# Cross-attention with LoRA, one core: value and denominator matmuls as one run, key stacks split for four heads and placed through memory

## The reference, cut to what matters

```python
# x (16, 112, 1024), ctx (16, 375, 1024); H = 1024, NH = 32 heads, NKV = 8 key heads, HD = 32, R = 16
def lora(x, W, A, B): return x @ W + 2.0 * (x @ A @ B)
q = lora(x, Wq, Aq, Bq)          # 32 heads of 32
k = lora(ctx, Wk, Ak, Bk)        # 8 heads of 32, each shared by 4 query heads
v = lora(ctx, Wv, Av, Bv)
scores = einsum('bhqd,bhtd->bhqt', q, k) / sqrt(32)
attn = softmax(scores, axis=-1)
context = einsum('bhqt,bhtd->bhqd', attn, v)
out = x + lora(context, Wo, Ao, Bo)
```

## Time and profile of the kernel before

| what | value |
|---|---|
| median of 3 runs | 1053.68 us (1049.55 to 1054.18) |
| the profiled execution | 1055.77 us, its span 1054.0 us |
| TensorE busy, matmuls / weight loads | 992.0 us (94%) / 783.7 us (74%) |
| VectorE, ScalarE, GpSimd busy | 583.9, 496.7, 286.2 us |
| mean granted clock of TensorE | 0.982 of full speed |
| chain of work that ended last | TensorE 79%, VectorE 7%, ScalarE 6% |

### The profile page before, as it was taken

One profiled execution on the slowest core, in us unless ns is written; L12 is line 12 of the kernel. 1 busy time (PEld: TensorE's weight loads), 2 busy tenths in 40 slices (PEclk: granted clock), 3 DMA queues, 4 the chain that ended last, 5 costly groups with the idle time before them and its releaser, 6 DMA issues.

```text
span 1054.0 us, 17987 instructions
## 1 busy us (share of the span) xinstructions
PE 992.0 (94%) x5904; PEld 783.7 (74%) x5904; DVE 583.9 (55%) x1005; ACT 496.7 (47%) x971; POOL 286.2 (27%) x84
## 2 busy tenths in 40 slices
PE   6989999999999999999999999999999857999998
PEld 5879999887777777777777777777777424678886
DVE  5661221387666666666666667666667555323331
ACT  3341221436656657666666666666667433201000
POOL 1201000002334434434433533533543435300000
PEclk9999999999999999999999999999999887999999
DMA  6729523462513513423323323324322340667652
GB/s 188 238 81 247 174 70 105 121 155 59 130 46 87 123 46 94 108 58 94 95 71 94 95 71 94 95 61 104 95 53 56 90 129 31 167 206 216 195 163 80
DMA packets 104436, 118.13 MB, mean 112 GB/s; under 512 B 29536, under 2 KB 89056, under 8 KB 104400
## 3 DMA queue, kind: packets, MB, share of 16 engines
q1 hardware_dynamic: 100540, 104.00, 37.2%
q10 hardware_dynamic: 3860, 13.67, 3.6%
HBM read 87.59 MB, written 29.82 MB: 111 GB/s over the span
## 4 chain that ended last, share of the span: by engine, by line
PE 79%; DVE 7%; ACT 6%; issue 4%; DMA 3%; ACTq 0%; SPq 0%; POOL 0%; DVEq 0%; POOLq 0%
PE ps L664 12%; PE ps L666 12%; PE ps L665 12%; PE ps L854 9%; PE ps L869 8%; PE ps L843 7%; PE ps L749 4%; PE ps L804 3%; PE ps L808 3%; PE ps L806 3%; PE ps L905 3%; ACT probs L1038 2%; ACT k_stack L978 1%; DVE ct_lo L1169 1%; DMA out_dram<-residual 1%
## 5 line engine op out<-in xcount | busy, mean ns | idle before, releaser
L1247 DVE TENSOR_REDUCE maxima<-ps 112x1 f32<-112x375 f32 x512 | 270.8, 543 | 107.6 <-PE ps L854 101.1
L1038 ACT ACTIVATE probs<-ps 125x448 f32<-125x448 f32 x384 | 206.9, 544 | 134.1 <-PE ps L843 130.3
L645 POOL TENSOR_TENSOR prob_sum<-probs 125x1792 f32<-125x1792 f32 x32 | 129.3, 4042 | 380.5 <-ACT probs L1038 380.5
L854 PE MATMUL ps<-k_stack,q_stack 96*112 96x376 f32 x512 | 188.9, 369 | 7.4 <-DVE maxima L1247 5.8
L843 PE MATMUL ps<-q_stack,k_stack 97*125 97x448 f32 x384 | 147.6, 385 | 13.8 <-ACT probs L1038 13.5
L854 PEld LDWEIGHTS ps<-k_stack,q_stack 96*112 96x112 f32 x512 | 90.5, 177 | 86.5 <-DVE maxima L1247 69.5
L650 POOL TENSOR_TENSOR prob_sum<-prob_sum,probs 125x1792 f32<-125x1792 f32 x32 | 129.1, 4033 | 34.4 <-ACT probs L1038 34.4
L978 ACT ACTIVATE k_stack<-ps 32x376 fp32r<-32x376 f32 x256 | 121.6, 475 | 9.9 <-PE ps L666 6.0
L804 PE MATMUL ps<-wv_hi,ct_hi 128*125 128x256 f32 x384 | 112.1, 292 | 0.5 <-DVE k_stack L1174 0.5
L808 PE MATMUL ps<-wv_hi,ct_lo 128*125 128x256 f32 x384 | 108.1, 281 | 0.0
L806 PE MATMUL ps<-wv_lo,ct_hi 128*125 128x256 f32 x384 | 108.0, 281 | 0.0
(11 more groups left out here) (80 smaller groups left out, 1477.0 us busy)
## 6 DMA issues: line engine op xcount, KB each, us to landing
ctx_in<-in_ctx_dram SPq DMA_DIRECT2D x16, 1344.0 KB
q_stack<-q_scratch SPq DMA_DIRECT2D x96, 224.0 KB, 3.6
x_in<-in_x_dram SPq DMA_DIRECT2D x8, 896.0 KB, 8.4
q_scratch<-q_out_hi SPq DMA_DIRECT2D x16, 448.0 KB, 2.8
q_scratch<-q_out_lo SPq DMA_DIRECT2D x16, 448.0 KB, 3.7
attn_scratch<-attn SPq DMA_DIRECT2D x32, 224.0 KB, 3.7
attn_rows<-attn_scratch SPq DMA_DIRECT2D x14, 512.0 KB, 4.6
inv_tile<-inv_scratch SPq DMA_DIRECT2D x56, 128.0 KB, 5.0
```

Of the source, the lines that this page charges most:

```text
L854: mm = pe.matmul(ps[0:NQ, NAT + i % 2, 0:NTE], qst[nxt][0:STK, g, rr * NQ:(rr + 1) * NQ], kst[nxt][0:STK, g, :], start=True, stop=True)
L1038: act.activation(probs[:, c, j, :], ps[0:TR, score_bank(i), 0:QH], ACT.Exp, scale=SM).then_inc(exp_done, 1)
L1247: dve.tensor_reduce(maxima[:, h, i:i + 1], ps[0:NQ, NAT + i % 2, 0:NT], AX.X, ALU.max).then_inc(max_done, 1)
```

## The change

1. The three P pieces and D of a half-batch become one P piece late in the half-batch (0.815 of its cost): 12 value matmuls in chunk order and then the four denominators of the same half-batch. D stays as the place where ScalarE copies the denominators and SP stores them, at the start of the next half-batch.
2. GpSimd adds `probs` per head: eight additions of 448 columns instead of two of 1792.
3. A half-batch's four key heads are split by one ScalarE copy and one VectorE subtraction over all 128 partitions into new tiles `k_out_hi`, `k_out_lo`. SP stores both to a new scratch in memory (`store_k`, at F0 and F1), waits for the stores, and loads the high part twice and the low part once into the stack (`load_k`, at G0 and G1). N of that half-batch waits for the loads. The stores of the second four heads come at the end of the second half-batch, their loads in the first half-batch after it.
4. The plan: S and N are due earlier, and S alternates between two banks from the first pair on.
5. ScalarE's wait for the stored queries moves ahead of the steps.

```diff
-S_IN_DEN = (3, 5, 7, 9, 11)
+S_IN_DEN = (1, 3, 5, 7, 9, 11)
 PLAN = sorted(
-    [("S", i, 0.01 + 0.07 * i) for i in range(TC * JH)]
-    + [("P", 0, 0.31), ("P", 1, 0.583), ("P", 2, 0.925), ("A", 0, 0.048), ("D", 0, 0.097)]
+    [("S", i, 0.01 + 0.065 * i) for i in range(TC * JH)]
+    + [("A", 0, 0.005), ("D", 0, 0.005), ("P", 0, 0.815)]
     + [("I", 0, 0.35), ("J", 0, 0.45)]
-    + [("N", i, 0.03 + 0.052 * i) for i in range(JH * RH)] + [("M", 0, 0.925)]
-    + [("E0", j, 0.62 + 0.08 * j) for j in range(JH)] + [("E1", j, 0.03 + 0.06 * j) for j in range(JH)]
-    + [("F0", j, 0.62 + 0.08 * j) for j in range(JH)] + [("F1", j, 0.03 + 0.06 * j) for j in range(JH)],
+    + [("N", i, 0.02 + 0.045 * i) for i in range(JH * RH)] + [("M", 0, 0.805)]
+    + [("E0", 0, 0.55), ("F0", 0, 0.55), ("G0", 0, 0.75), ("E1", 0, 0.82), ("F1", 0, 0.82), ("G1", 0, 0.12)],
...
+        if piece[0] == "K" and piece[2] == KC - 1:
+            early = [item for item in order if item[0] in (f"E{piece[1]}", f"F{piece[1]}", f"G{piece[1]}")]
+            order = [item for item in order if item not in early] + early
...
+            def store_k(b, half):
+                sp.wait_ge(k_lo_set, 2 * b + half + 1)
+                for hl, t in ((0, kev_hi[half]), (1, kev_lo[half])):
+                    sp.dma_start(k_scr[hl, bass.ds(b, 1), half, :, :].rearrange("b p n -> p (b n)"),
+                                 t[:, :].bitcast(F32)).then_inc(k_stored[half], 16)
+            def load_k(b, par, half):
+                sp.wait_ge(k_stored[half], 32 * (b + 1))
+                for n, hl in enumerate((0, 0, 1)):
+                    sp.dma_start(kst[par][HD * n:HD * (n + 1), half * JH:(half + 1) * JH, :].bitcast(F32),
+                                 k_scr[hl, bass.ds(b, 1), half, :, :].rearrange("b (j d) n -> d (b j) n", d=HD)
+                                 ).then_inc(k_in[half][par], 16)
...
+                        elif kind == "F0":
+                            store_k(b + 2, 0)
+                        elif kind == "G0":
+                            load_k(b + 2, off % 2, 0)
+                        elif kind == "F1":
+                            store_k(b + 2, 1)
+                        elif kind == "G1":
+                            load_k(b + 1, (off + 1) % 2, 1)
...
                             if i == 0:
                                 pe.wait_ge(q_in[h][nxt], 48 * (pair + (off + 1) // 2 + 1))
-                                pe.wait_ge(k_lo_set, JH * (m + 1))
+                                pe.wait_ge(k_in[h][nxt], 48 * (pair + (off + 1) // 2 + 1))
...
-                            pe.wait_ge(exp_done, NS * n + JH * (i + 1))
-                            if i == 0:
-                                at_least(pe, attn_set, n)
-                                pe.wait_ge(v_set, 2 * (b + 1))
-                            for j in range(JH):
...
-                        elif kind == "D":
-                            denominators(n - 1)
+                            pe.wait_ge(exp_done, NS * (n + 1))
+                            at_least(pe, attn_set, n)
+                            pe.wait_ge(v_set, 2 * (b + 1))
+                            for c in range(TC):
+                                for j in range(JH):
+                                    g = h * JH + j
+                                    mm = pe.matmul(ps[HD * j:HD * (j + 1), CTX, 0:QH],
+                                                   v_sb[cur][:, c, g * HD:(g + 1) * HD], probs[:, c, j, :],
+                                                   start=(c == 0), stop=(c == TC - 1))
+                                mm.then_inc(pv_done, 1)
+                            denominators(n)
...
-            def k_hi(b, par, half, j):
+            def k_hi(b, half):
                 act.wait_ge(k_done, 2 * b + half + 1)
-                at_least(act, st_done, NS * (2 * (b - 2) + half + 1))
-                for quad in range(2):
-                    op = act.activation(kst[par][HD * quad:HD * (quad + 1), half * JH + j, :],
-                                        ps[HD * j:HD * (j + 1), (VA, TURN)[half], 0:NTE], ACT.Copy)
-                op.then_inc(k_hi_set, 1)
+                at_least(act, k_stored[half], 32 * b)
+                act.activation(kev_hi[half][:, :], ps[:, (VA, TURN)[half], 0:NTE], ACT.Copy).then_inc(k_hi_set, 1)
...
-            def k_lo(b, par, half, j):
-                dve.wait_ge(k_hi_set, NKV * b + half * JH + j + 1)
-                dve.tensor_tensor(kst[par][2 * HD:3 * HD, half * JH + j, :],
-                                  ps[HD * j:HD * (j + 1), (VA, TURN)[half], 0:NTE],
-                                  kst[par][0:HD, half * JH + j, :], ALU.subtract).then_inc(k_lo_set, 1)
+            def k_lo(b, half):
+                at_least(dve, st_done, NS * (2 * (b - 2) + half + 1))
+                dve.wait_ge(k_hi_set, 2 * b + half + 1)
+                dve.tensor_tensor(kev_lo[half][:, :], ps[:, (VA, TURN)[half], 0:NTE], kev_hi[half][:, :],
+                                  ALU.subtract).then_inc(k_lo_set, 1)
```

More of the change, by code:

```diff
@@ L43 @@
 NS = TC * JH
+SUMS = 2 * JH
 NN = JH * RH
@@ L113, in half_order @@
         at += COST[piece[0]]
+        if piece[0] == "K" and piece[2] == KC - 1:
+            early = [item for item in order if item[0] in (f"E{piece[1]}", f"F{piece[1]}", f"G{piece[1]}")]
+            order = [item for item in order if item not in early] + early
     order += [(kind, i, 0) for kind, i, _ in plan]
-    assert "K" not in has or order.index(("K", 0, KC - 1)) < order.index(("E0", 0, 0))
+    for half in range(HALVES if "K" in has else 0):
+        assert order.index(("K", half, KC - 1)) < order.index((f"E{half}", 0, 0))
     return order + [("E", 0, 0)]
@@ L222, in xattn_kernel @@
         raw2, wsum2, ast2, bst2, at = staging("_o", r_x)
+        kev_hi, kev_lo = [None, None], [None, None]
+        for half in range(HALVES):
+            kev_hi[half], at = place(f"k_out_hi{half}", [P, NTE], F32R, at)
+            kev_lo[half], at = place(f"k_out_lo{half}", [P, NTE], F32R, at)
         assert at <= top[0]
@@ L289, in xattn_kernel @@
         k_lo_set = sem("k_lo_set")
+        k_stored = [sem("k_stored0"), sem("k_stored1")]
+        k_in = [[sem(f"k_in{h}{par}") for par in range(2)] for h in range(HALVES)]
         v_done = sem("v_done")
@@ L568, in step @@
                         elif kind == "D":
+                            if "G" in has[h]:
+                                at_least(sp, den_stored, 16 * 2 * b)
                             store_den(sp, 2 * b + h - 1, b - 1 + h, 1 - h)
@@ L744, in turn_ctx @@
                 elif k == 0:
-                    pe.wait_ge(k_lo_set, NKV * b)
+                    pe.wait_ge(k_lo_set, 2 * b)
                 else:
@@ L901, in denominators @@
             def denominators(n):
-                pe.wait_ge(psum_added, 2 * n + 2)
+                pe.wait_ge(psum_added, SUMS * (n + 1))
                 for j in range(JH):
@@ L912, in _ @@
             run_steps(pe, step, wo_factors)
-            denominators(2 * B - 1)
             def tile(pair, par):
@@ L1072, in wo_factors @@
             def wo_factors():
-                for par in range(2):
-                    act.wait_ge(q_stored[par], GROUPS * QS // 2 * 32)
                 ab_hi(W_O, CTX)
+            for par in range(2):
+                act.wait_ge(q_stored[par], GROUPS * QS // 2 * 32)
             run_steps(act, step, wo_factors)
```

45 lines of the change are left out of this document (20 added, 25 removed).

## The result

| | before | after | change | forecast |
|---|---|---|---|---|
| median, us | 1051.62 (1048.17 to 1054.18, 4 runs) | 1126.08 (1122.36 to 1129.55, 4 runs) | ratio 1.0705 [1.0672, 1.0737] | 1110 (1044 to 1128) |
| span of the profiled execution, us | 1054.0 | 1123.5 | +69.5 | +56 |
| first N starts, us | 210.51 | 230.60 | +20.1 | 230.1 |
| one batch in the loop, us | 40.21 | 44.32 | +4.1 | +3.0 |
| its first half (V), its second half (K), us | 20.56, 19.65 | 25.71, 18.61 | +5.2, -1.0 | |

The 69.5 us lie in four places: 20.1 until the first N, 6.0 from there to these twelve batches, 49.3 in them, and -5.9 behind them.

What follows compares the result with a forecast made beforehand. The prediction took TensorE, busy 97 to 99% in the loop, as the bound. From the profiled 1055.8 us: -23.5 - 4 + 20 + 41.6 + 22.1 = 1112, less 2.1 for the median: 1110 us, range 1044 to 1128.

Steps and rivals of the forecast that it cites:

- case A: The forecast itself: TensorE waits for keys at N0 and the clock falls behind it; 1110 us, chance 0.50.
- Merged run: Four TensorE bursts become one run of 3.47 us, saving 0.81 us in each of 29 half-batches: -23.5 us.
- Keys split once: Loop: a 0.97 us TensorE stall per batch goes, about 1 us of waits for maxima comes; -4 us net.
- The wait at N0: First half-batch's first N waits 3.2 us for keys through memory, in 13 batches: +41.6 us (21 to 62).
- Its cause: Key stores, ready at 12.7 us, stand behind the 1.5 MB context load in SP's one queue until 17.0.
- rival C: In the loop the keys are in place before N0, so only the prologue pays: 1046 us, chance 0.13.
- The clock: Behind each wait at N0, 3.4 us at half speed cost 1.7 us, 13 times: +22 us, from nothing to double.
- Prologue: Batch 0's keys are stored behind nine query loads; first N moves from 210.51 to 230.1: +20 us (18 to 23).
- The end: Half-batches at the run's end: no term of its own; the last three of 32 wait for other engines.
- B: The wait comes but the clock stays, or half the wait and the clock falls half as often: 1088, chance 0.22.
- D: Keys are in place in the loop and the prologue's keys pass too: 1026 us, chance 0.12.
- E: Column-tiled weight loads cannot overlap the group ahead, so the merged run costs 38 us: 1148, chance 0.03.

Runs made afterwards that it cites:

- e8: Kernel after with context load behind key loads, first keys' prologue transfers ahead of the second context load, and an earlier key split: 1019.34 us, 0.9695 of before.
- e9: Key path of e8, split due at 0.5 and loads at 0.62, with the kernel before's four bursts and due times: 1037.07 us, 0.9883 of before.
- e1: Kernel after with its merged run and new due times, but keys split per head in place, slightly earlier than before: 1067.72 us, 1.0137 of before.
- e5: e1 with N and M at the due times of the kernel before: 1070.35 us, 1.0184 of before.
- e7: Kernel after with the first four heads' key stores issued from ScalarE's queue instead of SP's: 1120.57 us, 1.0659 of before.
- e2: Kernel after with the context load issued behind the key loads on SP: 1052.19 us, 1.0024 of before.
- e3: Kernel after with 23 unused filler matmuls ahead of the wait at N0 in the first half-batch: 1101.44 us, 1.0482 of before.

## Why the forecast came out as it did

The forecast's case A happened, in the right places and order, and 1126 lies in its range, near the upper end. That it lies so near is in part luck: gains were under-sized by 0.9 us a batch and losses by 1.8, and the two errors partly cancel. Per batch it had -1.6 - 0.3 + 3.2 + 1.7 = +3.0 us; the runs give -1.8 - 1.0 + 4.3 + 2.4 = +3.9, and +4.1 was measured. Point by point:

- **Merged run: right, slightly under-sized.** The run's groups start every 0.376 us (0.40 forecast). From start to start the run takes 3.14 us, and the step from M into it 0.19, which holds M's own time: 3.33 together (3.47). e8 against e9, which holds the new due times and the earlier split too: 1.81 us a batch, 0.905 a half-batch (0.81).
- **Keys split once: the stall of 0.97 us went as said; what was mis-sized is what it was netted against.** The forecast set about 1 us of new waits for maxima against it and came to -0.3 a batch; no such wait exists in the loop of the kernel after or of e8, and e9 against the kernel before gives -1.00. That this relief is also what makes the merge pay (e1, e5) the forecast did not see: it added the two as independent terms, which the sum allowed only because the change contains both.
- **The wait at N0: right in kind, 4.3 us in place of 3.2.** In the batch shown, counted from the first K (510.38): context load at 9.3 (9.5 forecast), the stores' landing and the loads' issue at 19.4 (19.0), N0 at 24.1 (23.1), since the loads took 4.7 us (4.1). N0 was also ready sooner, at 19.3 (19.9).
- **Its cause: half right.** The text put the stores' delay down to SP's one queue, and rival C would have had the keys in place on a free queue. e7 disproves that: from another queue they take nearly as long (5.4 and 5.8 us, against 5.9 and 6.3). e2 shows that with the context load issued later they land in 1.9.
- **The clock: right that it falls, wrong in how long.** The low stretch is 6.8 us, not the 3.4 of the earlier trace rows; e3 prices it at 2.4 us a batch in place of 1.7. The text had this doubling as the upper end.
- **Prologue: right.** First N at 230.60 against 230.1. Not foreseen was how uneven the waits about the loop's start are: of 14 behind a context load (13 of 3.2 us were counted) the first, ahead of the loop, left TensorE idle for 7.1 us and the second, in the loop's first batch, for 1.7.

```profile
230.60 0.63 PE L893 MATMUL ps<-k_stack,q_stack 96*112 96x376 f32 x1 [20.31 <-DMA k_stack<-k_scratch]
```

- **The end: under-sized.** Behind the twelve batches 5.9 us came back, where the forecast has little more than the merge's 0.81 for each of three half-batches. What of the rest is the due times was not tried.
- **Rivals.** B (clock stays) is e3's state, at 1101 (forecast 1088, with a smaller wait). D (both placements right) was priced at 1026, and e8 with an earlier split gives 1019. E, weight loads exposed in the run, falls: behind the first eight, the next four weight loads are issued in 0.13 us at the start of each group, and the groups keep 0.376 us where exposed loads would have added to the 0.40. The rule that the forecast named beside it (the Trainium skill, "TensorE: Matmul & The Clock Gate", Part 3: Packing small matmuls — row/col tiling) is not borne out by this trace. The timeline of weight loads in the run:

```profile
525.85 0.16 PEld L908 LDWEIGHTS ps<-probs,v 125*32 125x32 f32 x8 [0.27 <-issue]
526.25 0.13 PEld L908 LDWEIGHTS ps<-probs,v 125*32 125x32 f32 x4 [0.25 <-issue]
526.62 0.13 PEld L908 LDWEIGHTS ps<-probs,v 125*32 125x32 f32 x4 [0.25 <-issue]
```

## What to carry to other kernels

A detour through memory costs what is ahead of it on the transfer engines, here from SP's queue and from ScalarE's alike: before adding one, list the large loads issued in the microseconds ahead and move them behind it (74 us here, by three lines). A TensorE saving that gathers work into one long run can starve the engines that live on its other results; here it paid only once these had fewer small per-head steps queued ahead of what TensorE waits for. When two parts of a change are added up, try each without the other: here the same merge cost 0.7 to 0.95 us a batch with one key split and gave 1.81 with the other.

## What the runs showed of the hardware

- Two key stores of 188 KB landed 1.9 us after their issue without a large load ahead (e2); behind the 1.5 MB context load 5.9 and 6.3 us after it from the same queue (after), 5.4 and 5.8 from another (e7).
- A wait of TensorE of 4.7 us went with 6.8 us at 0.50, from 2.2 us ahead of its end on (after). One of 2.30 us was followed by 3.4 us at 0.50 (e2). Two waits of 0.4 and 1.1 us, 1.6 us apart, were followed by the same in three batches of e5 and left the clock at 1.00 in the others, as N0's waits of 0.8 us in e2 and the filled wait of e3 did.
- A run of column-tiled groups advances by 0.376 us a group of four (0.40 the first, 0.49 the last), and the step from M into it takes 0.19 us, M's own time included (after).
